# A gated four-layer stack on one core: rebuilt stretches between the attention flows, maxima rows written ahead of halves, a Newton step kept in PSUM, and norms split over two engines

## What is computed

```python
x = x + tanh(g_xattn[0]) * rope_causal_attention(norm(x), ctx)        # 16 heads of 8
x = x + tanh(g_ffn[0])   * node_network(norm(x))                      # 6 nodes, 8 heads of 16
x = x + tanh(g_xattn[1]) * cross_attention(norm(x), ctx)              # 16 heads of 64, norms again inside
x = x + tanh(g_ffn[1])   * quantised_gated_ffn(norm(x))               # 128 -> 352 -> 128
x = x + tanh(g_xattn[2]) * causal_attention(norm(x), ctx, mask)       # 16 heads of 8
x = x + tanh(g_ffn[2])   * quantised_relu_ffn(norm(x))                # 128 -> 512 -> 128
x = x + tanh(g_xattn[3]) * biased_attention(norm(x), ctx)             # 16 heads of 8
x = x + tanh(g_ffn[3])   * expert_layer(norm(x))                      # 32 experts, top 2, fixed capacity
```

## Time and profile before

| | |
|---|---|
| time, median of 3 runs | 1889.33 us (1886.15 to 1894.91) |
| the profiled execution | 1894.12 us, span 1892.3 us, mean granted clock 0.857 |
| PE busy | 1303.1 us, 69% of the span |
| DVE busy | 1224.2 us, 65% |
| ACT busy | 836.7 us, 44% |
| POOL busy | 476.5 us, 25% |
| DMA | 108.2 MB, mean 57 GB/s |

### The profile page before, as it was taken

One profiled execution on the slowest core, in us unless ns is written; L12 is line 12 of the kernel. 1 busy time (PEld: TensorE's weight loads), 2 busy tenths in 40 slices (PEclk: granted clock), 3 DMA queues, 4 the chain that ended last, 5 costly groups with the idle time before them and its releaser, 6 DMA issues. The chain is left out here.

```text
span 1892.3 us, 32152 instructions
## 1 busy us (share of the span) xinstructions
PE 1303.1 (69%) x12243; PEld 922.7 (49%) x12245; DVE 1224.2 (65%) x2458; ACT 836.7 (44%) x1294; POOL 476.5 (25%) x650
## 2 busy tenths in 40 slices
PE   0798179999999991499899882179833688530674
PEld 0465056666666660366666650146622455320674
DVE  5665337777777777666776756836657577558444
ACT  1255226676776771355555532225513156410330
POOL 6343232222222201222222222134310200000452
PEclk9999579999999996599999996579965789965787
DMA  2243312222222222000000000122101122143434
...
DMA packets 115782, 108.20 MB, mean 57 GB/s; under 512 B 44766, under 2 KB 99230, under 8 KB 114590
## 3 DMA queue, kind: packets, MB, share of 16 engines
...
q0 software_dynamic: 2048, 2.65, 0.6%
...
...
## 5 line engine op out<-in xcount | busy, mean ns | idle before, releaser
L595 ACT ACTIVATE Pt<-bank 128x1024 f32<-128x1024 f32 (+1 forms) x384 | 366.4, 954 | 176.3 <-PE bank L539 174.7
L651 DVE TENSOR_REDUCE l0f_Mf<-bank 128x4 f32<-128x1024 f32 x192 | 234.5, 1221 | 108.8 <-PE bank L518 108.8
L559 PE MATMUL bank<-Pt,V 128*32 128x256 f32 (+1 forms) x3072 | 196.9, 375 | 10.7 <-POOL Pt L400 9.5
L1127 POOL TENSOR_TENSOR Psum<-Pt 128x512 f32<-128x512 f32 x64 | 83.5, 1305 | 269.8 <-ACT Pt L1259 269.8
L400 POOL TENSOR_SCALAR_AFFINE_SELECT Pt<-Pt 128x512 f32<-128x512 f32 x128 | 81.9, 640 | 176.1 <-ACT Pt L595 176.1
L559 PEld LDWEIGHTS bank<-Pt,V 128*32 128x32 f32 x3072 | 81.5, 111 | 82.3 <-issue 26.2
L416 POOL CAST parts<-nodes 128x256 fp32r<-128x256 f32 x96 | 38.4, 400 | 306.5 <-PE bank L490 306.5
L539 PE MATMUL bank<-l0f_QK 64*128 64x256 f32 x768 | 97.6, 333 | 19.4 <-DMA l0f_QK<-l0f_NMrow 18.9
L841 PE MATMUL bank<-ident,Qf 128*128 128x128 f32 x64 | 14.4, 418 | 140.2 <-SPq L243 91.6
L1297 DVE TENSOR_TENSOR qk_lo<-bank,qk_hi 128x512 fp32r<-128x512 f32 x64 | 44.2, 690 | 99.3 <-ACT qk_hi L1251 99.3
L651 DVE TENSOR_REDUCE l2x_Mf<-bank 128x4 f32<-128x1024 f32 x64 | 76.9, 1221 | 32.3 <-PE bank L518 32.2
...
...
## 6 DMA issues: line engine op xcount, KB each, us to landing
...
```

What stands on the lines that cost most here:

```text
L559: last = pe.matmul(bank[4][32 * x:32 * x + 32, o + q0:o + S], Va[:, 2 * n + k, 4 * j + x, :], Pp[:, (f + x // 2) % 4, x % 2, k * S:k * S + ...
L595: act.activation(Pp[:, g % 4, :, 0:w], banks[:, 2:4, 0:w], ACT.Exp, scale=L.scale).then_inc(exp_done, 1)
L651: d.tensor_reduce(m, A.rearrange("p h (t k) -> p h t k", t=2), AX, ALU.max).then_inc(max_done, 1)
L1127: e.tensor_tensor(Psum[:, q % 2], Pp[:, q % 4, :, 0:S], Pp[:, q % 4, :, S:2 * S], ALU.add).then_inc(key_sum, 1)
```

## The change

It has these parts:

1. **Prologue and `l0x` setup**: the loads of the heads, the context, the rope table and the constant rows (`rowk`, now one tile for all flows) come first, and `X` later; the rotation of the keys moves from POOL to DVE, in two pieces placed where DVE waits for PE; POOL clears `V` before the loads; all blank rows of `QK` are written by ACT (`slots_blank`), some of them before the loads are awaited.
2. **`l0f` setup**: weight scalings move from POOL to DVE. At its end the bias row is added to `X` by POOL behind its flow, and gain and gate are one DVE instruction.
3. **Events**: `N` of the unit in front now stands ahead of `L` at j = 2 of `l0f`. In the other flows the two never stand at the same j.
4. **`l1x` setup**: loads and ACT's high parts move ahead of the barrier that ends `l0f`; the two norms in a row become one (`eps` 1e-10, `scale` 1 + 1e-5); POOL makes only the first low parts before the barrier, and the rest (16 pieces of 128 columns, `Esel`, 7 of 256) behind it, with a count `w_lo` that PE waits on.
5. **Norms shared** (end of `l0f`, `l1x`, both quantised layers, experts): DVE scales 8 tiles and ACT the other 8, with scale and bias from per-partition columns. The norms ahead of `l0f`, `l2x` and L3 stay on DVE alone.
6. **Newton step**: its first product goes back into the PSUM bank instead of the SBUF tile `st1`.
7. **`l2x` and L3 setup**: `V` is filled by ACT, and the mask rows `padr` are made by DVE; both were POOL's.

```diff
-                if j == (2 if self.node else 3) and ok(z):
-                    out.append(("L", z, 0))
                 if j == 0 and ok(b):
                     out.append(("N", b, 1))
                 if j == half and ok(a):
                     out.append(("N", a, 0))
+                if j == (2 if self.node else 3) and ok(z):
+                    out.append(("L", z, 0))
...
-        def ln_dve(v, src, dst, eps):
+        def ln_dve(v, src, dst, eps, scale=1.0, shared=True):
...
-            rstd_dve(v, var, NT, eps, 1.0)
-            for t in range(NT):
+            rstd_dve(v, var, NT, eps, scale)
+            half = NT // 2 if shared else NT
+            if shared:
+                v.link(d.scalar_tensor_tensor(out=st2[:, NT:2 * NT], in0=m, scalar=-1.0, in1=st3[:, 0:NT],
+                                              op0=ALU.mult, op1=ALU.mult))
+                d.drain().then_inc(ln_ask, 1)
+            for t in range(half):
...
+            if shared:
+                d.wait_ge(ln_answer, v.count("ln"))
+
+        def ln_act(a, src, dst):
+
+            rstd_act(a, NT)
+            a.eng.wait_ge(ln_ask, a.count("ln"))
+            for t in range(NT // 2, NT):
+                last = a.eng.activation(dst[:, t, :], src[:, t, :], ACT.Identity, scale=st3[:, t:t + 1],
+                                        bias=st2[:, NT + t:NT + t + 1])
+            last.then_inc(ln_answer, 1)
...
-        def queries_blank(g, L):
-
-            for r in range(L.ring):
-                g.eng.tensor_copy(L.QK[:, r, :, 0, :], bc(L.rowk[:, 0:1].unsqueeze(1), [P, L.blocks, S]))
...
+        def slots_blank(a, L, which):
+
+            for k in which:
+                r, x = k // 2, k % 2
+                a.eng.copy(L.QK[:, r, :, x, :], bc(rowk[:, x:x + 1].unsqueeze(1), [P, L.blocks, S]))
...
         def setup_sp(s):
             e = s.eng
-            e.dma_start(X[:], x_rows).then_inc(dma_in, 16)
+            e.dma_start(tA[:], T["x_heads"]).then_inc(dma_in, 16)
+            e.dma_start(ctxS[:], T["ctx_heads"]).then_inc(dma_in, 16)
+            e.dma_start(rope[:], T["c_rope"]).then_inc(dma_in, 16)
+            e.dma_start(rowk[:], T["c_rows"]).then_inc(dma_in, 16)
...
             d.tensor_reduce(st1[:], xs, AX, ALU.add).then_inc(mean_ask, 1)
+            rotate(v, ctxS[:], Kf[:], tB[:], (0,))
             d.wait_ge(mean_full, 1)
...
             d.tensor_reduce(st1[:], sq, AX, ALU.add).then_inc(mean_ask, 1)
+            rotate(v, ctxS[:], Kf[:], tB[:], (1,))
             d.wait_ge(mean_full, 2)
...
-            queries_blank(g, L0f)
-            for c in range(6):
-                e.tensor_tensor(WeS[:, c], WeS[:, c], bc(ew[:, 3 * c:3 * c + 1], [P, D]), ALU.mult)
-                g.link(e.tensor_tensor(Wn[:, 3, c], Wn[:, 3, c], bc(actw[:, c:c + 1], [P, D]), ALU.mult))
...
             flow_pool(g, L0f, bases[1])
+            g.link(e.tensor_tensor(lng[:, 1], lng[:, 1], bc(gates[:, 4:5], [P, D]), ALU.mult))
+            g.link(e.tensor_tensor(X[:], X[:], bc(lng[:, 1].unsqueeze(1), [P, NT, D]), ALU.add))
...
-            rstd_act(a, NT)
+            ln_act(a, Qf, Qf)
...
+                d.tensor_scalar(WeS[:, c], WeS[:, c], ew[:, 3 * c:3 * c + 1], None, ALU.mult)
+                d.tensor_scalar(Wn[:, 3, c], Wn[:, 3, c], actw[:, c:c + 1], None, ALU.mult)
...
-            v.link(d.tensor_tensor(Qf[:], Qf[:], bc(lng[:, 0].unsqueeze(1), sh_), ALU.mult))
-            v.link(d.tensor_tensor(Qf[:], Qf[:], bc(lng[:, 1].unsqueeze(1), sh_), ALU.add))
-            v.link(d.scalar_tensor_tensor(out=X[:], in0=Qf[:], scalar=gates[:, 4:5], in1=X[:],
-                                          op0=ALU.mult, op1=ALU.add))
+            v.link(d.scalar_tensor_tensor(out=Qf[:], in0=Qf[:], scalar=gates[:, 4:5],
+                                          in1=bc(lng[:, 0].unsqueeze(1), sh_), op0=ALU.mult, op1=ALU.mult))
+            v.link(d.tensor_tensor(X[:], Qf[:], X[:], ALU.add))
...
+        def l1x_in_act(a):
+            act = a.eng
+            loaded(a, 8)
+            act.copy(wt_hi[:, 2048:3072], wF[:, 2048:3072]).then_inc(split_hi, 1)
+            for c in range(2):
+                act.copy(ctxH[:, 1024 * c:1024 * c + 1024], ctxF[:, 1024 * c:1024 * c + 1024]).then_inc(split_hi, 1)
+            for c in range(2):
+                act.copy(wt_hi[:, 1024 * c:1024 * c + 1024], wF[:, 1024 * c:1024 * c + 1024]).then_inc(split_hi, 1)
...
             g.barrier()
+            e.wait_ge(split_hi, 5)
+            pick = Rden[:, 0, 0:8]
+            for k in range(8):
+                for x in range(2):
+                    low(wt_lo, wF, wt_hi, slice(1024 * x + k * P, 1024 * x + (k + 1) * P))
...
+            for b in range(1, B):
+                low(ctxL, ctxF, ctxH, slice(b * S, (b + 1) * S))
...
                     pe.wait_ge(lo_done, 4 + g)
+                    if g < 8:
+                        pe.wait_ge(w_lo, 5 + 2 * g + (g > 1))
...
-            ln_dve(v, X, Qf, 1e-5)
-            ln_dve(v, Qf, Qf, 1e-5)
+            ln_dve(v, X, Qf, 1e-10, 1.0 + 1e-5)
...
-                    near, t = Dinv[:, g % 2, 1], st1[:]
-                    d.scalar_tensor_tensor(out=t, in0=y[:, S:2 * S], scalar=-1.0, in1=near, op0=ALU.mult,
+                    near, t, den = Dinv[:, g % 2, 1], st1[:], y[:, S:2 * S]
+                    d.scalar_tensor_tensor(out=den, in0=den, scalar=-1.0, in1=near, op0=ALU.mult,
                                            op1=ALU.mult).then_inc(pair_done, 1)
                     d.wait_ge(pair_done, 3 * g + 1)
-                    d.scalar_tensor_tensor(out=t, in0=t, scalar=2.0, in1=near, op0=ALU.add,
+                    d.scalar_tensor_tensor(out=t, in0=den, scalar=2.0, in1=near, op0=ALU.add,
                                            op1=ALU.mult).then_inc(pair_done, 1)
...
+            slots_blank(a, L, range(2))
             rstd_act(a, NT)
             loaded(a, len(x_loads(k)))
-            keys_blank(a, attentions[k])
+            slots_blank(a, L, range(2, 5))
+            if k == 2:
+                a.eng.copy(v_view(L)[:, :, :, 0:L.dh], Kf[:].rearrange("p t (h d) -> p t h d", d=L.dh))
+                slots_blank(a, L, range(5, 6))
...
+            if k == 2:
+                d.tensor_scalar(padr[:], padi[:], 1.0, MASKED, ALU.is_equal, ALU.mult)
```

More of the change, by code:

```diff
@@ L712, in setup_pool @@
         def setup_pool(g):
+            g.eng.memset(ones[:], 1.0)
+            g.link(g.eng.memset(V[:], 0.0))
+            values_ones(g, L0)
             loaded(g, N_IN)
-            g.link(g.eng.memset(ones[:], 1.0))
             g.barrier()
@@ L730, in loaded, with rotate @@
             seat.eng.wait_ge(dma_in, 16 * seat.count("in", n))
-        def rotate(seat, src, dst, tmp):
+        def rotate(seat, src, dst, tmp, js=(0, 1)):
             e = seat.eng
-            for j in range(2):
+            for j in js:
                 def part(ap, o):
@@ L1156, in l1x_pe @@
                         pe.wait_ge(nm_free, u - 1)
+                    if j == 0 and u < 2:
+                        pe.wait_ge(w_lo, 2 + u)
+                    elif j == 0 and r == 0:
+                        pe.wait_ge(w_lo, 20 + b)
                     c = 2 * H1 * DH1 + r * 512
@@ L1231, in l1x_act @@
             act = a.eng
-            rstd_act(a, NT)
-            rstd_act(a, NT)
-            loaded(a, 8)
+            ln_act(a, X, Qf)
             a.link(act.activation(g1[:], g1[:], ACT.Tanh))
-            for c in range(3):
-                act.copy(wt_hi[:, 1024 * c:1024 * c + 1024], wF[:, 1024 * c:1024 * c + 1024]).then_inc(split_hi, 1)
-            for c in range(2):
-                act.copy(ctxH[:, 1024 * c:1024 * c + 1024], ctxF[:, 1024 * c:1024 * c + 1024]).then_inc(split_hi, 1)
             a.barrier()
@@ L1724, in x_dve @@
             L = attentions[k]
-            ln_dve(v, X, Qf, 1e-5)
+            ln_dve(v, X, Qf, 1e-5, shared=False)
             loaded(v, len(x_loads(k)))
```

110 lines of the change are left out of this document (49 added, 61 removed).

## The result

The changed kernel takes 1815.57 us (median of 4 runs, 1814.29 to 1825.83), the kernel before 1891.38 on the same occasion: ratio 0.961, 95% interval 0.957 to 0.966. The forecast was 1819, range 1801 to 1832. The profiled execution has a span of 1813.0 us, 79.3 less than before's 1892.3; the sum said 70.0. I cut both spans at the same events (first instruction of each stretch or flow); these are differences of start times in the two timelines.

The account below looks back on a forecast made before the run. PE was taken as near full inside the flows, losing time only to its own waits, and nearly idle between them, where stretch length counts whole. Terms summed to -70.0 us: 1894.1 to 1824.1, 1819 as median, range 1801 to 1832.

Parts of the forecast that it names:

- the sum: Whole kernel: all priced parts of the change added together, -70.0 us.
- Seven terms of stretches between flows: Prologue -10.2, setups of `l0f` -5.4, `l1x` -23.4, `l2x` -12.7, L3 -4.9; gated layer +0.6, other quantised layer -0.8 us.
- forecast -5.4: Setup of `l0f`: weight scalings on DVE let PE begin at 233.7 instead of 239.10.
- DVE's reduction of 2.29 (L795): Prologue: read as a 2048-column instruction's time where POOL is still, against 4.01 beside POOL's rotation.
- second rival: `l1x`: POOL's low-part splits beside DVE come late for the first projection, +7 us, 1826; chance 0.15.
- `l0f` flow, forecast -1: Row moved ahead of L: DMA wait goes, stall moves to U; -2.5 us, less +1.8 at `W` turns, taken as -1.
- of 0.39 it leaves 0.06: `l0f` flow: gain per unit after 0.33 of stall moves to U; x 41 units = -2.5 us.
- The first rival: `l0f` flow: U isn't held and the 18.9 us go nearly whole, 16 more, 1803; chance 0.16.
- Newton step, forecast -11.4: `l1x`: with the PSUM bank as operand, each of 15 waits on `G` shortens by 0.76 us.
- The long kind: `l1x`: second Newton product beside POOL's addition, near 1.2 us at pairs PE waits for, against a mean of 809 ns.
- the 0.8 forecast: Experts' norm: shared scalings, 3.35 against 4.2 us, -0.8.
- The objection to halves: Shared norms: DVE's eight scalings need 2.1 and wait 1 us for ACT; a 10 to 6 split would be even.

Follow-up runs that it names:

- e6: Changed kernel with all of POOL's low parts made ahead of the `l1x` barrier again: 1823.5 us, ratio 0.964 to the kernel before.
- e4: Changed kernel with both rows of event N in `l0f` written by ACT instead of DVE: 1801.0 us, ratio 0.953 to the kernel before.
- e3: Changed kernel with the Newton step's first product back in the SBUF tile: 1825.8 us, ratio 0.966 to the kernel before.
- e12: Kernel of e3 with POOL's addition of 128x512 written as two of 128x256: 1804.2 us, ratio 0.963 to the kernel before.
- e8: Changed kernel with `padr`, the mask rows of `l2x`, made by POOL again: 1816.3 us, ratio 0.963 to the kernel before.
- e7: Changed kernel with four unread ACT copies added ahead of the `l2x` barrier: 1821.1 us, ratio 0.964 to the kernel before.
- e1: Control: the changed kernel once more, no edit: 1814.8 us, ratio 0.961 to the kernel before.
- e10: Changed kernel with eleven of sixteen scalings of the shared norms on DVE, five on ACT: 1801.3 us, ratio 0.961 to the kernel before.

## Why the prediction was right

The time came out 3.4 us under the forecast and inside the range, and the main waits went where the prediction said. That it is so near is in part luck. The medians show 75.8 us gained, the two profiled executions 79.3, and the sum said 70.0: `l0f` gave 5.4 and `l1x` 3.9 more than their terms, while `l2x` (5.0 better) and the experts (6.4 worse), for whose clock the sum had no term, nearly cancel.

**Prologue, setups, norms.** Seven terms of stretches between flows, most priced from quiet rows of the same instruction, lie within 1.3 us. The largest miss is `l0f`'s setup (-6.7, forecast -5.4): the last load released DVE 15.0 us behind the stretch's start and not 15.5, and PE began 2.9 behind it, not 3.7, as DVE's twelve scalings of 0.28 started 0.2 apart. In the prologue one reading was wrong and cost nothing: DVE's reduction of 2.29 (L795) ran beside POOL's fills, so it shows no quiet POOL; the addition of 2.29 in the earlier trace rows does. The clash of loads and splits behind the barrier (second rival) did not come: no wait on a low part shows, and e6 shows that nothing of the move is given back.

**`l0f` flow, forecast -1, measured -6.4.** The mechanism was right: the stall moves to U. At a clock of 1.00 in both the edit gives 5.0 to 5.3; about 1.1 of the 6.4 is the clock of the flow's lead. The term that was mis-sized is "of 0.39 it leaves 0.06" a unit: it left some 0.17, the typical unit going from 8.96 to 8.79 us. The gain was priced by PE's idle gap, 0.39, and is 0.46 between starts. The loss, priced at 0.33, is 0.30: the gap of 0.22 to 0.23 in 39 units and the 0.07 by which an unheld product overlaps the one ahead. I let the row hold DVE for its whole 0.40, but the next instruction starts 0.33 behind it. Summed between starts over the whole window it is -18.1 ahead of B, +11.2 ahead of the closing product and +1.6 ahead of W: -5.3, with nothing left open. The first rival (PE quite free) was false here; e4 had to take the row off DVE for it.

**Newton step, forecast -11.4, measured -13.0 (e3).** The long kind was sized rightly, "near 1.2": ahead of the 15 waits the product took 1.17 to 1.26 before and 0.42 after, which is 0.79 a time in the mean. The waits fell by 12.6, 0.84 a time; the 0.05 between isn't traced. Taking the long kind instead of the mean was what made it right; the mean would have given 6. The Trainium skill (Advanced Engine Details and Errata, GPSIMD Details) has GpSimd share a read and a write interface with VectorE, in conflict with VectorE instructions that have two SBUF inputs or run in a 2-port mode. e3 and e12 agree with the first, and e12 shows the size: one POOL instruction. The scaling held in e8 has one SBUF tensor and a column of scalars; whether it ran in such a mode no run here shows.

**What the sum left out.** `l2x` -5.0 and the experts +5.6 against a forecast of 0 and -0.8. The first is granted clock, and e7 shows that it isn't bought by a shorter stretch. Of the second 4.8 is clock. The norm of the experts gained 0.7, near the 0.8 forecast. The experts took 245.7 to 254.2 in the profiled runs of e1 to e8. `l1x` had 2.3 more than e3 explains; in kernels not edited there it takes 346.0 at a clock of 0.96 and 350.0 at 0.94, so part of that can be clock, and the rest is open.

**The shared scalings.** Taken 0.38, measured 0.40. The 0.385 estimated from the figures of the Trainium skill (ScalarE: Activation LUTs, What ACT_TABLE_LOAD costs) lies near. The objection to halves that the prediction drew from that estimate was borne out in part: e10's eleven to five is better by some 2.9 us of stretches, and halves against VectorE alone gain 1.0 where no table load follows and lose 0.4 where one does.
